# Taking the soft-MoE logits from PSUM on VectorE together with their row maximum

## What is computed

```python
phi_n = phi * rsqrt(sum(phi**2, axis=0) + 1e-6)
logits = einsum('bmd,npd->bmnp', x, phi_n)              # x: (2, 1024, 192), phi_n: (64, 16, 192)
D = softmax(logits, axis=1)                             # over the 1024 tokens of a sequence
C = softmax(logits.reshape(bsz, m, n * p), axis=-1)     # over the 1024 slots
Xs = einsum('bmd,bmnp->bnpd', x, D)                     # what each slot reads
hdn = layernorm(Xs) @ w1 + b1; hdn = gelu(hdn); Ys = hdn @ w2 + b2     # 64 experts of 16 slots
Y = einsum('bsd,bms->bmd', Ys, C)
```

## Time and profile before

| | us |
|---|---|
| median of 3 runs | 557.95 |
| the three runs | 543.9, 557.96, 557.95 |
| the profiled execution | 550.43 |
| its span, first to last instruction | 548.3 |
| mean granted TensorE clock in it | 0.942 of full |

### The profile page before, as it was taken

How to read it: one execution, slowest core, us unless ns; L and a number is a source line. 1 busy time by engine, 2 the same in 40 slices (tenths; PEclk the granted TensorE clock), 3 DMA queues, 4 the chain that set the end, 5 groups by cost and what they waited for, 6 DMA issues and landing times.

```text
span 548.3 us, 8490 instructions
## 1 busy us (share of the span) xinstructions
PE 463.9 (85%) x3158; PEld 374.1 (68%) x3158; DVE 336.7 (61%) x771; ACT 212.3 (39%) x392; POOL 171.4 (31%) x256
## 2 busy tenths in 40 slices
PE   0279999879849999999996998595994979999996
PEld 0146776669638888888885777484881547777785
DVE  1967676258572588787663368966965215555576
ACT  0155572029834433434332575356641122221120
POOL 6755478037210054221112224503151032222210
PEclk9999999789989999999997998898897889999999
DMA  6610000000500000000002400006003999998114
GB/s 119 151 29 2 2 1 2 1 0 2 96 16 1 0 1 0 1 2 1 1 0 79 181 1 1 0 7 253 1 0 122 426 377 389 384 389 327 35 33 115
DMA packets 18938, 48.63 MB, mean 89 GB/s; under 512 B 6354, under 2 KB 13618, under 8 KB 14802
## 3 DMA queue, kind: packets, MB, share of 16 engines
q1 hardware_dynamic: 12594, 42.37, 22.0%
q0 software_dynamic: 2912, 3.37, 2.4%
q10 hardware_dynamic: 3392, 2.36, 1.4%
HBM read 44.92 MB, written 3.15 MB: 88 GB/s over the span
## 4 chain that ended last, share of the span: by engine, by line
PE 66%; DVE 14%; ACT 6%; issue 5%; DMA 4%; POOL 3%; SPq 1%; POOLq 0%; DVEq 0%; ACTq 0%
PE ps L1010 9%; PE ps L855 7%; PE ps L962 4%; PE ps L906 4%; PE ps L987 2%; PE ps L841 2%; PE ps L998 2%; PE ps L887 2%; DMA ys_dram<-ysb 2%; DMA ys<-ys_dram 1%; PE ps L888 1%; PE ps L889 1%; PE ps L815 1%; PE ps L890 1%; PE ps L670 1%
## 5 line engine op out<-in xcount | busy, mean ns | idle before, releaser
L1010 PE MATMUL ps<-ys,ct 128*128 128x192 f32 x256 | 49.6, 345 | 2.1 <-DMA ys<-ys_dram 2.1
L1723 DVE SCALAR_TENSOR_TENSOR res<-ps,riC,res 128x192 f32<-128x192 f32 x128 | 46.4, 412 | 7.1 <-PE ps L1010 4.6
L855 PE MATMUL ps<-pr,et 128*128 128x192 f32 x256 | 47.8, 340 | 1.2 <-DVE et L1561 0.7
L1010 PEld LDWEIGHTS ps<-ys,ct 128*128 128x128 f32 x256 | 38.9, 188 | 12.5 <-issue 5.5
L855 PEld LDWEIGHTS ps<-pr,et 128*128 128x128 f32 x256 | 42.7, 195 | 4.2 <-ACT et L1164 3.3
L530 POOL DMA_DIRECT2D ys<-ys_dram x32 | 19.7, 619 | 78.4 <-PE ps L1010 46.8
L440 POOL TENSOR_SCALAR ve<-mv 128x1 f32<-128x1 f32 x32 | 11.1, 348 | 91.7 <-DVE mv L1576 69.0
L1245 ACT ACTIVATE hs<-ps 128x384 f32<-128x384 f32 x16 | 7.9, 491 | 77.8 <-PE ps L962 77.8
L1714 DVE COPY ysb<-ps 128x192 f32<-128x192 f32 x16 | 5.7, 358 | 50.0 <-PE ps L987 50.0
L1157 ACT ACTIVATE zz<-zz,nmx 128x1024 f32<-128x1024 f32 x16 | 18.4, 1152 | 36.6 <-DVE nmx L1555 36.6
L1619 DVE TENSOR_TENSOR top<-top,ec 128x1024 f32<-128x1024 f32 x12 | 23.8, 1980 | 13.4 <-ACT ec L1208 13.4
(11 more groups left out here) (354 smaller groups left out, 1271.0 us busy)
## 6 DMA issues: line engine op xcount, KB each, us to landing
w1r<-in_p_w SPq DMA_DIRECT2D x16, 1152.0 KB, 16.7
w2r<-in_p_w SPq DMA_DIRECT2D x16, 1152.0 KB, 13.5
ys_dram<-ysb ACTq DMA_DIRECT2D x16, 96.0 KB, 8.0
ys<-ys_dram POOLq DMA_DIRECT2D x32, 48.0 KB, 6.9
phn<-in_L_ffn_phi SPq DMA_DIRECT2D x1, 768.0 KB, 7.1
out<-res SPq DMA_DIRECT2D x4, 192.0 KB, 3.4
out<-res ACTq DMA_DIRECT2D x4, 192.0 KB, 4.0
wp<-in_L_tok_W_proj SPq DMA_DIRECT2D x1, 384.0 KB, 7.2
```

The costliest lines, as they stand in the source:

```text
L855: last = mm(d[:, 0:D], et[:, k, :], pr[:, b * KT + k, 0:D], start=(k == 0), stop=(k == KT - 1))
L1010: mm(bank(5 + q % 3)[:, 0:D], ct[:, u % 2, k, :], ys[:, t % YR, b, :], start=True, stop=True).then_inc(m["yp_filled"], 1)
L1723: v.scalar_tensor_tensor(res[:, i, :], bank(5 + q % 3)[:, 0:D], riC[:, i:i + 1], res[:, i, :], ALU.mult, ALU.add).then_inc(m["yp_taken"], 1)
```

## The change

VectorE takes each tile's logits out of PSUM, with one instruction that adds a zero, writes the sum to `ec` and the maximum of the row to `mxC`. `mxC` is a view of the statistics tile `mv`, which is free by then. A second, small instruction negates it into `nmC`. ScalarE's copy and VectorE's separate `tensor_reduce` are gone. `l_copied` now comes from VectorE. The new order for a tile is `x2_lo(i + 1)`, the shifts as before, `l_take(i)`, `l_top(i)`, for all 16 tiles. There is one more memset, of the zero, ahead of the stage.

```diff
+    LOWEST = -3.0e38
...
+        zero = sb("zero", [P, 1])
...
+        mxC = mv[:, :, 0]
...
-            def l_copy(i):
-                act.wait_ge(m["l_filled"], i + 1)
-                sc.copy(ec[:, i, :], bank(logit_bank(i), 2)).then_inc(m["l_copied"], 1)
-
...
-                l_copy(i)
...
+            v.memset(zero[:], 0.0)
...
-            def l_max(i):
+            def l_take(i):
+                dve.wait_ge(m["l_filled"], i + 1)
+                v.tensor_tensor_reduce(ec[:, i, :], bank(logit_bank(i), 2), bc(zero[:], [P, NS]), 1.0, LOWEST, ALU.add,
+                                       ALU.max, mxC[:, i:i + 1]).then_inc(m["l_copied"], 1)
                 dve.wait_ge(m["l_copied"], i + 1)
-                v.tensor_reduce(nmC[:, i:i + 1], ec[:, i, :], AX, ALU.max, negate=True).then_inc(m["lmax_ready"], 1)
+                v.tensor_scalar(nmC[:, i:i + 1], mxC[:, i:i + 1], -1.0, None, ALU.mult).then_inc(m["lmax_ready"], 1)
 
             def l_top(i):
                 b, k = divmod(i, KT)
                 if k == 0:
                     return
-                dve.wait_ge(m["l_copied"], i + 1)
...
+                l_take(i)
                 l_top(i)
-                if i >= KT:
-                    l_max(2 * (i - KT))
-                    l_max(2 * (i - KT) + 1)
```

## The result

The changed kernel takes 556.37 us (median of 12 runs, 552.47 to 559.51), the kernel before 552.65 (12 runs, 543.9 to 557.96): +3.7 us, 0.7%. The ratio given with the result is 1.0153, 95% interval 1.0103 to 1.0203. It leaves out the slower of the runs of before, and so is higher than the ratio of the medians, 1.0067. Either way it is a small loss, whose interval just reaches 2%. The profiled execution took 552.47 us against 550.43, with a span of 550.4 against 548.3.

What follows compares the result with a forecast made beforehand. TensorE, busy 85% of the span, bounds it; the end moves with the second all-reduce, which waits for tile 15's maximum. Terms of 2.02 and 0.44 us add 2.46: 550.43 becomes 552.9 us, range 546 to 566.

Steps and rivals of the forecast that it cites:

- the dispatch: After the first all-reduce: TensorE's first dispatch waits for tile 10's take and starts at 338.0 instead of 333.02.
- the one long maximum of tile 11: VectorE's maximum of tile 11 stands until GpSimd's six subtractions are done, about 8 us, ending at 354.51.
- the second all-reduce 2 to 3 us later: End of the logits loop: GpSimd's second all-reduce and all behind it move by 2.46 us.
- The fused instruction: VectorE's new take of each tile: 1.37 us, bounds 1.24 and 2.45; 1.48 from its start to the maximum's.
- rival C: Fused instruction slow, 2.45 us on nine takes: +16.0 us, 566.4; decides for slower from 1.9 us a take; chance 0.09.
- VectorE bound in batch 0: Batch 0's tiles: VectorE needs 3.02 us a tile against TensorE's 2.68; tile 7's maximum ends 2.49 us later.
- The race: After the first all-reduce: tile 10's maximum starts before GpSimd's first subtraction, by a margin of 0.07 to 0.72 us.
- the sum: All terms to the second all-reduce: 2.02 us at tile 13's logits and 0.44 at the last tile, +2.46 us.
- tile 13: Its logits start at 356.23 instead of 354.21, +2.0 us, and TensorE takes 4.46 us for it as before.
- The tail: From the second all-reduce to the end: distance unchanged.
- the stall that was there: TensorE's 6.09 us wait before tile 13, behind the blocked maximum of tile 11: swallows nearly all 5 us of dispatch delay.
- Rival E: A VectorE maximum gets in between two of GpSimd's subtractions: -2.7 us, 547.7; chance 0.06.

Runs made afterwards that it cites:

- e2: Kernel before, with GpSimd's six subtractions of batch 0 moved to VectorE: 547.94 us, ratio 1.0002.
- f1: Kernel before, with GpSimd waiting for its own subtraction of batch 0 before it issues the next: 545.93 us, ratio 0.9952.
- e5: Changed kernel, with the first dispatch waiting only for tile 9's take and the k = 1 shift behind tile 10's maximum: 545.32 us, ratio 0.9897.
- f2: Changed kernel, with GpSimd waiting for its own subtraction of batch 0 before it issues the next: 552.49 us, ratio 1.0054.

## Why the prediction was right, and where not

**Right.** The sign and the size of the total: no change that counts, +2.46 us said, +2.0 between the profiled executions, +3.7 between the medians. The time lay in the range of 546 to 566. The forecast's own, narrower range of 559 to 562 it missed: that was set from the three runs shown, whose median was 5 us above that of 12. The ratio of 1.0045 lies below the measured interval. Of the signs named, the takes, the first all-reduce, the dispatch and the one long maximum of tile 11 came as said; the second all-reduce 2 to 3 us later and the unchanged distance from there to the end did not.

**The fused instruction.** Said 1.37 (1.24 to 2.45), measured 1.21 with 0.08 for reading the accumulator; from the take's start to the maximum's 1.32, not 1.48. The lower bound was the better one, and rival C (1.9 us or more) had no ground.

**VectorE bound in batch 0.** Right: 2.85 us a tile, where 3.02 was said. `ctop` came at 331.21, for which I had said 331.25; that is partly luck. The six pitches took 17.1 us instead of 18.1, but tile 1 was filled 1.1 us late (take at 308.07, copy at 306.94 before), with a clock of 0.83 from 304 to 310 where it had been 1.00. In the other profile the all-reduce was 26.6 us behind F instead of 27.8, so this costs 1.1 to 2.4 us over the two profiles of each kernel.

**The race.** Right: the maximum of tile 10 at 337.70, GpSimd's first subtraction at 338.06; dispatch at 337.74 (said 338.0); the last subtraction ends at 352.99 (353.43), the blocked maximum at 354.07 (354.51), logits 13 at 355.75 (356.23).

**The stage, 2.1 to 2.5 us shorter than the sum.** The sum puts the second all-reduce 73.6 us behind F (71.14 and 2.46), and it came at 71.1 and 71.5. In the profiled execution the mis-sized term is tile 13, for which I carried over 4.46 us at a clock of 0.50. The clock was 1.00 from 354 to 377, and the next take starts at 358.36, 2.6 us after the logits do. TensorE had paused 1.73 us, not the 3.1 of the sum (353.1 to 356.23), because the first dispatch, behind a pause of 4.43 us, had itself run slowly (5.49 us, with a clock of 0.50 from 340 to 343; 4.23 in the earlier trace rows). In the second profile of the changed kernel the half clock did come at tile 13:

```profile
360.57 0.60 PE L890 MATMUL ps<-ph,X2H 128*128 128x512 f32 x1 [2.40 <-DVE mv L1604]
```

The clock was 0.50 from 361 to 364, and the take of tile 13 came 4.15 us behind its logits, close to the 4.46. There the sum was missed further forward: the first all-reduce came 26.6 us behind F, where the sum has 27.8. So the tile behind this pause cost 2.6 us in one execution and 4.2 in the other, and two don't show which is the rule.

**The tail, which I had at nothing.** From the second all-reduce to the end it took 177.0 us (177.3 in before's second profile), and 179.1 and 180.4 in the changed kernel. In the first pair of profiles, 0.6 us is GpSimd's idle of 7.51 instead of 6.88. Another 0.9 is TensorE at the start of batch 1's dispatch, with a clock of 0.77 from 387.3 to 391 before and of 0.50 in the changed kernel; the last 0.6 I did not trace. Before, then changed:

```profile
383.38 1.63 PE L906 MATMUL ps<-x2b,ls_low 128*128 128x193 f32 x4 [6.79 <-DVE xs L1653]
...
387.38 2.35 PE L906 MATMUL ps<-x2b,ls_low 128*128 128x193 f32 x8 [0.38 <-DVE xs L1653]
389.56 1.91 PE L917 MATMUL ps<-ident,xs 128*128 128x128 f32 x16
```
```profile
383.97 1.63 PE L909 MATMUL ps<-x2b,ls_low 128*128 128x193 f32 x4 [7.70 <-DVE xs L1654]
...
387.98 2.94 PE L909 MATMUL ps<-x2b,ls_low 128*128 128x193 f32 x8 [0.38 <-DVE xs L1654]
390.71 2.26 PE L920 MATMUL ps<-ident,xs 128*128 128x128 f32 x16
```

The pause in front is 0.9 us longer. The change moves 0.3 of that: the last logits now end that much earlier than the all-reduce. Whether this makes the clock come back later as a rule, or these are two draws, the runs don't show: over all kernels GpSimd's idle went from 6.78 to 8.00 us whatever the edit, and the tail from 177.0 to 180.9, with 179.9 in e2 and 178.1 in f1, which don't have the change. That the total's misses cancelled, -2.5 in the stage and +2.1 behind it, is chance.

**The step that failed in the argument**, though the forecast held. "So 5 us of delay at the dispatch is nearly all swallowed by the stall that was there." The stage was even, as that says, but I took the stall's end for given by GpSimd's last subtraction. It is so only while the maximum is issued late in a row of subtractions. e5 moved the dispatch 4 to 5 us and gained 9; f1 and f2 ended the stall in both kernels and left 4.5 us between them. That the changed kernel's own maximum was issued third in the row was not foreseen as something that mattered, so that its stage came out even is in part luck. Rival E was rejected on one row, the one at 341.20; one instance can't show that something never happens.

## What to carry to other kernels

A copy moved to the busier engine is not priced by its duration but by what stands behind it in that engine's queue, here the operands of the next tile and a release that another engine waits for. When a change comes out even, look for the stall that hides it: that stall can be the larger prize, and here a single wait took 8 us from the stage, though the total was too scattered to show it. And run the unchanged kernel as a control before a ratio within 1% is believed.

## What the runs showed of the hardware

A maximum of VectorE, with both inputs in SBUF, did not run beside a subtraction of GpSimd: either it was held up (10.31 us instead of 1.22 in before) or the next subtraction was (3.40 instead of 2.40). A low part or a take, with one input in PSUM, ran beside GpSimd at its usual 0.29 and 1.23 us. The Trainium skill (SBUF — State Buffer, Who interferes with whom) says that two SBUF inputs contend with GpSimd's reads, and the same page (SBUF: two separate sides) that the loser waits for the whole instruction. By that rule a maximum would wait at most one subtraction, 2.4 us. Rows here show 10.31, 11.75, 6.67, 7.34, 6.96 and 5.73 us, several instructions of GpSimd in a row; with a wait between them the longest maximum was 3.26 us, and a shift took 3.45. By what rule VectorE stays shut out over a row was not settled: the count above (first unhindered, or a later one) fits ten cases of ten, and no more is shown.

The idle behind each partition all-reduce, with nothing to wait for in the profile, was 6.78 to 8.00 us behind the second one in 14 profiles, different from run to run at the same place.
